# One-hots and first norm on other engines, an earlier store of the first rows, and two gathers in the other order, in a one-core layer of gated cross-attention and experts

## The reference

```
h    = layernorm(x)
q    = h @ Wq.T;  k, v = split(ctx @ Wkv.T)
# each token sees 4 rows of its batch's context: seg, seg-1, seg-2, seg-3
x    = x + tanh(g_xattn) * (softmax(q.k / 4 over the 4 rows, 16 heads) @ v) @ Wo.T
h    = layernorm(x)
p    = softmax(h @ gate_w.T); the 2 best of 8 experts
x    = x + tanh(g_ffn) * sum over them of p_e * (silu(h @ w1[e] + b1[e]) @ w2[e] + b2[e])
```

## Time and profile before

| | us |
|---|---|
| median of 3 runs | 359.64 (359.12 to 360.45) |
| the profiled execution | 359.07 |
| its span | 357.4 |
| TensorE, matmul, busy | 325.2 (91%) |
| VectorE busy | 268.8 (75%) |
| GpSimd busy | 213.9 (60%) |
| ScalarE busy | 175.9 (49%) |

### The profile page before, as it was taken

How to read it: one execution, slowest core, us unless ns; L and a number is a source line. 1 busy time by engine, 2 the same in 40 slices (tenths; PEclk the granted TensorE clock), 3 DMA queues, 4 the chain that set the end, 5 groups by cost and what they waited for, 6 DMA issues and landing times.

```text
span 357.4 us, 11383 instructions
## 1 busy us (share of the span) xinstructions
PE 325.2 (91%) x3440; PEld 269.0 (75%) x3440; DVE 268.8 (75%) x629; ACT 175.9 (49%) x495; POOL 213.9 (60%) x243
## 2 busy tenths in 40 slices
PE   8586999999999899999999999999999999999930
PEld 7455778998888688788888888888888887778720
DVE  5376899999998967878878788787887876666620
ACT  3252255555465467555565555655546553252400
POOL 4677788987675061474738747386574865662430
PEclk9897899999999989999999999999999999999985
DMA  6679999999899821122323223232332323242211
GB/s 197 203 244 420 399 422 402 415 364 406 289 386 381 271 62 33 30 40 42 61 47 51 50 43 62 47 47 48 46 61 49 48 47 62 34 65 26 33 19 14
DMA packets 31582, 53.30 MB, mean 149 GB/s; under 512 B 4882, under 2 KB 25730, under 8 KB 29476
## 3 DMA queue, kind: packets, MB, share of 16 engines
q0 software_dynamic: 9408, 26.63, 28.8%
q1 hardware_dynamic: 17700, 23.10, 18.1%
q10 hardware_dynamic: 4416, 2.80, 2.6%
HBM read 42.36 MB, written 10.17 MB: 147 GB/s over the span
## 4 chain that ended last, share of the span: by engine, by line
PE 68%; DVE 16%; issue 4%; DMA 4%; POOL 3%; ACT 2%; SPq 0%; ACTq 0%; POOLq 0%; DVEq 0%
PE ps L1246 28%; PE ps L1260 16%; PE ps L1263 8%; DVE ps L1433 4%; PE ps L1274 2%; DMA sel<-near_rows,win_near 2%; PE ps L1268 2%; PE ps L960 2%; DVE w_parts L1429 2%; PE ps L1072 2%; PE ps L1081 2%; DMA w_parts<-in_itok_BxS 2%; DVE sel L1429 2%; PE ps L1267 1%; PE ps L1262 1%
## 5 line engine op out<-in xcount | busy, mean ns | idle before, releaser
L1246 PE MATMUL ps<-sel,w_parts 128*128 128x128 f16 x1776 | 141.7, 219 | 0.8 <-issue 0.7
L1246 PEld LDWEIGHTS ps<-sel,w_parts 128*128 x1776 | 119.4, 98 | 25.9 <-issue 1.4
L939 ACT ACTIVATE sel<-ps,b1T 128x128 f32<-128x128 f32 x296 | 84.3, 368 | 89.7 <-PE ps L1246 89.6
L686 POOL DMA_INDIRECT out<-sel x37 | 62.6, 1692 | 85.0 <-DVE sel L1721 69.9
L1260 PE MATMUL ps<-w_parts,sel 128*128 x259 | 96.3, 379 | 0.3
L1263 PE MATMUL ps<-w_parts,sel 128*128 x259 | 70.6, 273 | 0.0
L678 POOL DMA_INDIRECT sel<-tokens_split,sel x37 | 43.8, 1184 | 15.7 <-DVE sel L1644 9.2
L1676 DVE SCALAR_TENSOR_TENSOR sel<-sel 128x512 f16<-128x512 f32 x74 | 51.3, 693 | 2.5
L1662 DVE SCALAR_TENSOR_TENSOR w_parts<-w_parts (+1 forms) x32 | 39.0, 1220 | 10.4 <-issue 7.2
L673 POOL TENSOR_TENSOR sel<-sel 128x1 f32<-128x1 f32 x37 | 40.2, 1086 | 2.9 <-PE ps L1274 2.9
L1674 DVE TENSOR_SCALAR sel<-sel 128x512 f16<-128x512 f32 x74 | 33.8, 456 | 8.7 <-ACT sel L939 8.2
(11 more groups left out here) (244 smaller groups left out, 479.3 us busy)
## 6 DMA issues: line engine op xcount, KB each, us to landing
w_parts<-in_L_ffn_w SPq DMA_DIRECT2D x16, 1024.0 KB, 11.4
out<-xs SPq DMA_DIRECT2D x16, 128.0 KB, 8.0
tokens_split<-xsplit ACTq DMA_DIRECT2D x13, 128.0 KB, 5.8
xs<-in_x SPq DMA_DIRECT2D x3, 512.0 KB, 8.8
near_rows<-w_parts SPq DMA_DIRECT2D x4, 256.0 KB, 6.9
sel<-tokens_split,sel POOLq DMA_INDIRECT x37, 3.0
out<-sel POOLq DMA_INDIRECT x37
w_parts<-in_L_xattn_Wkv SPq DMA_DIRECT2D x1, 512.0 KB, 4.2
```

The source lines that it names most:

```text
L686: pool.indirect_dma_start(out_rows, bass.IndirectOffsetOnAxis(slot_row[:, at(q - 1)], 0), y_sb[(k + 3) % 4], None, compute_op=ALU.add).the ...
L939: act.activation(h32[n][:, c * P:c * P + P], ps_h[n][:, c * P:c * P + P], ACT.Silu, bias=biases[:, c:c + 1], scale=1.0 / (X_SCALE * W_SCALE))\
L1246: mm = pe.matmul(ps_h[n][:, c * P:c * P + P], w, xx, start=(i == 0), stop=(i == len(products) - 1))
```

## The change

VectorE makes the one-hots, behind its flag and ahead of the token statistics of tiles 1 to 7. GpSimd's first work on data is now the first norm of tile 0, and then its part of b2. b2 is loaded on ScalarE's queue behind the tokens of batch 0, and ScalarE's copy of it stands ahead of its copies of Wkv. SyncE loads the segments for the one-hots ahead of Wkv, and the two gates, b1 and gate_w behind the tokens of batch 3. ScalarE stores the rows of batch 0. The rows of tile 1 are gathered ahead of those of tile 0. TensorE makes the first two picks, behind six spins, ahead of the transposes of Wq and the first turn, and ScalarE keeps them there.

```diff
@@ -390,8 +390,8 @@
         @block.sync
         def _(sp):
             sp.dma_start(segr_i[:, :], seg_tiles).then_inc(s["seg_in"], 16)
+            sp.dma_start(near_seg, seg_tiles[0:1, :].to_broadcast([P, P])).then_inc(s["near_in"], 16)
             sp.dma_start(wkv_raw, Wkv.rearrange("(o p) c -> p o c", p=P)).then_inc(s["wkv_in"], 16)
-            sp.dma_start(near_seg, seg_tiles[0:1, :].to_broadcast([P, P])).then_inc(s["near_in"], 16)
             sp.dma_start(wq_raw, Wq.rearrange("(o p) c -> p o c", p=P)).then_inc(s["wraw_in"], 16)
             sp.dma_start(ctx0[:, 1:B, :], ctx_first[:, 1:B, :]).then_inc(s["ctx_in1"], 16)
 
@@ -401,14 +401,6 @@
             tokens_in(1)
             sp.dma_start(wo_raw, Wo.rearrange("(o p) c -> p o c", p=P)).then_inc(s["wo_in"], 16)
             tokens_in(2)
-            sp.dma_start(gates[:, 0:1], g_xattn.rearrange("(o n) -> o n", o=1).to_broadcast([P, 1]))\
-                .then_inc(s["small_in"], 16)
-            sp.dma_start(gates[:, 1:2], g_ffn.rearrange("(o n) -> o n", o=1).to_broadcast([P, 1]))\
-                .then_inc(s["small_in"], 16)
-            sp.dma_start(b1_raw, b1.rearrange("e (c p) -> (e c) p", p=P)).then_inc(s["small_in"], 16)
-            sp.dma_start(gate_raw, gate_w).then_inc(s["small_in"], 16)
-            sp.dma_start(b2_raw, b2).then_inc(s["b2_in"], 16)
-
             def chunk(n, done, src, dst):
                 sp.dma_start(ctx_g, ctx_rows[bass.ds(src, P), :]).then_inc(s["g_ctx"], 16)
                 sp.wait_ge(s["g_kv"], n + 1)
@@ -434,9 +426,14 @@
                 sp.wait_ge(s["kv_ok"], b + 2)
                 sp.dma_start(kv_near[b], kv_sb[:, b, :]).then_inc(s[f"kv_out{b}"], 16)
 
-            near_out(0)
             sp.wait_ge(s["kv_out0"], 16)
             tokens_in(3)
+            sp.dma_start(gates[:, 0:1], g_xattn.rearrange("(o n) -> o n", o=1).to_broadcast([P, 1]))\
+                .then_inc(s["small_in"], 16)
+            sp.dma_start(gates[:, 1:2], g_ffn.rearrange("(o n) -> o n", o=1).to_broadcast([P, 1]))\
+                .then_inc(s["small_in"], 16)
+            sp.dma_start(b1_raw, b1.rearrange("e (c p) -> (e c) p", p=P)).then_inc(s["small_in"], 16)
+            sp.dma_start(gate_raw, gate_w).then_inc(s["small_in"], 16)
             near_out(1)
 
             def step(t):
@@ -523,16 +520,11 @@
             pool.iota(away_i[:, :], pattern=[[-1, WIN]], base=0, channel_multiplier=1).then_inc(s["away_ok"], 1)
             pool.wait_ge(s["away_ok"], 1)
             pool.tensor_copy(away[:, :], away_i[:, :]).then_inc(s["away_ok"], 1)
-            pool.wait_ge(s["near_in"], 16)
-            pool.tensor_copy(near_win, near_seg).then_inc(s["near_f"], 1)
-            pool.wait_ge(s["near_f"], 1)
-            pool.tensor_scalar(near_win, near_win, float(1 - WIN), 0.0, ALU.add, ALU.max).then_inc(s["near_w"], 1)
-            pool.wait_ge(s["near_w"], 1)
-            pool.wait_ge(s["away_ok"], 2)
-            for j in range(WIN):
-                pool.tensor_scalar(pick_hot[:, j, :], near_win, float(P - WIN), away[:, j:j + 1], ALU.min, ALU.is_equal)\
-                    .then_inc(s["hot_ok"], 1)
             first_norms(1, slice(0, 1))
+            pool.wait_ge(s["b2_hi_ok"], 1)
+            pool.tensor_scalar(b2_raw[:, :], b2_raw[:, :], 16.0, None, ALU.mult).then_inc(s["b2_lo_ok"], 1)
+            pool.wait_ge(s["b2_lo_ok"], 1)
+            pool.tensor_tensor(b2_lo[:, :], b2_raw[:, :], b2_hi[:, :], ALU.subtract).then_inc(s["b2_lo_ok"], 1)
             first_norms(2, slice(1, TPB))
             pool.wait_ge(s["win_ok"], 1)
             general = flag(pool)
@@ -599,15 +591,18 @@
                 pool.wait_ge(s["pick_ok"], 2)
                 pool.sem_inc(s["sel_k"], 1)
                 pool.wait_ge(s["kv_out0"], 16)
-                pool.indirect_dma_start(slot(0).rearrange("p j c -> p (j c)"), None, kv_near[0],
-                                        bass.IndirectOffsetOnAxis(win_near[:, 0:1], 0)).then_inc(s["sel_in0"], 16)
+                for u in (1, 0):
+                    pool.indirect_dma_start(slot(u).rearrange("p j c -> p (j c)"), None, kv_near[0],
+                                            bass.IndirectOffsetOnAxis(win_near[:, u:u + 1], 0))\
+                        .then_inc(s[f"sel_in{u}"], 16)
             with pool.Else():
                 pool.indirect_dma_start(slot(0).rearrange("p j c -> p (j c)"), None, kv_all,
                                         bass.IndirectOffsetOnAxis(win_all[:, 0:1], 0)).then_inc(s["sel_in0"], 16)
                 pool.wait_ge(s["sel_in0"], 16)
                 pool.wait_ge(s["pick_ok"], 2)
                 pool.tensor_scalar(keys_of(0), slot(0)[:, :, 0:D], 1.0, None, ALU.mult).then_inc(s["sel_k"], 1)
-            gather(1, 2)
+                pool.indirect_dma_start(slot(1).rearrange("p j c -> p (j c)"), None, kv_all,
+                                        bass.IndirectOffsetOnAxis(win_all[:, 1:2], 0)).then_inc(s["sel_in1"], 16)
             first_norms(3, slice(TPB, 2 * TPB))
             gather(2, 3)
             for t in range(T - 1):
@@ -620,10 +615,6 @@
                     first_norms(4, slice(2 * TPB, T))
                 elif t == 2:
                     gather(5, 6)
-                    pool.wait_ge(s["b2_hi_ok"], 1)
-                    pool.tensor_scalar(b2_raw[:, :], b2_raw[:, :], 16.0, None, ALU.mult).then_inc(s["b2_lo_ok"], 1)
-                    pool.wait_ge(s["b2_lo_ok"], 1)
-                    pool.tensor_tensor(b2_lo[:, :], b2_raw[:, :], b2_hi[:, :], ALU.subtract).then_inc(s["b2_lo_ok"], 1)
                 elif t == 3:
                     gather(6, 8)
                 elif 3 < t < T - 4:
@@ -696,11 +687,14 @@
             act.dma_start(ctx0[:, 0, :], ctx_first[:, 0, :]).then_inc(s["ctx_in0"], 16)
             act.dma_start(xs[:, 0:1, :], x_v[:, 0:1, :]).then_inc(s["x_first"], 16)
             act.dma_start(xs[:, 1:TPB, :], x_v[:, 1:TPB, :]).then_inc(s["x_in0"], 16)
+            act.dma_start(b2_raw, b2).then_inc(s["b2_in"], 16)
             act.wait_ge(s["consts"], 4)
             act.activation(var2[:, 0:1], half[:, 0:1], ACT.Copy).then_inc(s["unused"], 1)
             act.wait_ge(s["ctxT_ps"], 1)
             act.activation(ctxT[:, 0, :, :].rearrange("p k c -> p (k c)"), ps[:, 0, 0:256], ACT.Copy)\
                 .then_inc(s["ctxT_ok"], 1)
+            act.wait_ge(s["b2_in"], 16)
+            act.activation(b2_hi[:, :], b2_raw[:, :], ACT.Copy, scale=16.0).then_inc(s["b2_hi_ok"], 1)
             act.wait_ge(s["wkvT_ps"], 1)
             act.activation(WkvT[:, 0, 0:D], ps[:, 2, 0:D], ACT.Copy).then_inc(s["wkvT_ok0"], 1)
             act.wait_ge(s["wkvT_ps"], 2)
@@ -724,6 +718,8 @@
             act.wait_ge(s["seg_top_ok"], 1)
             first_x(0)
             keys_or_values(1)
+            act.wait_ge(s["kv_ok"], 2)
+            act.dma_start(kv_near[0], kv_sb[:, 0, :]).then_inc(s["kv_out0"], 16)
 
             general = flag(act)
 
@@ -803,12 +799,16 @@
                 act.wait_ge(s["shifts_ok"], n)
                 act.activation(r_ex[:, some, :], r_tmp[:, some, :], ACT.Exp).then_inc(s["rt_exp"], 1)
 
+            def picks_kept(h):
+
+                act.wait_ge(s["pick_ps"], h + 1)
+                act.activation(picked[:, 512 * h:512 * h + 512], ps[:, 2 + h, :], ACT.Copy).then_inc(s["pick_ok"], 1)
+
+            picks_kept(0)
             act.wait_ge(s["wT_ps"], 1)
             act.activation(WqT.rearrange("p k c -> p (k c)"), ps[:, 6, :], ACT.Copy).then_inc(s["wT_ok"], 1)
             first_turned(0)
-            for h in range(2):
-                act.wait_ge(s["pick_ps"], h + 1)
-                act.activation(picked[:, 512 * h:512 * h + 512], ps[:, 2 + h, :], ACT.Copy).then_inc(s["pick_ok"], 1)
+            picks_kept(1)
             first_x(1)
             first_turned(1)
             act.wait_ge(s["ctxT_ps"], 2)
@@ -827,9 +827,6 @@
             keys_values(2)
             act.wait_ge(s["small_in"], 64)
             act.activation(tanh_g[:, :], gates[:, :], ACT.Tanh).then_inc(s["gates_t"], 1)
-            act.wait_ge(s["b2_in"], 16)
-            act.activation(b2_hi[:, :], b2_raw[:, :], ACT.Copy, scale=16.0).then_inc(s["b2_hi_ok"], 1)
-
             def small_turned():
 
                 act.wait_ge(s["small_ps"], 1)
@@ -1028,10 +1025,6 @@
                         mm = pe.transpose(ps[:, bank, c * D + o * P:c * D + o * P + P], raw[:, o, c * P:c * P + P], ident[:, :])
                 mm.then_inc(s["wT_ps"], 1)
 
-            pe.wait_ge(s["seg_max_ok"], 1)
-            pe.wait_ge(s["wraw_in"], 16)
-            weight_turn(wq_raw, 6)
-
             def picks(h):
                 pe.wait_ge(s["kv_ok"], 1)
                 pe.wait_ge(s["hot_ok"], 2 * h + 2)
@@ -1112,8 +1105,12 @@
                     mm = pe.matmul(logits_at(u), x2T_at(u)[:, c, :], gateT[:, c, :], start=(c == 0), stop=(c == KC - 1))
                 mm.then_inc(s["logit_ps"], 1)
 
+            spin(6, 0)
+            picks(0)
+            pe.wait_ge(s["seg_max_ok"], 1)
```

(12 more changed lines are left out.)

## The result

| | us |
|---|---|
| the changed kernel, median of 20 runs | 360.75 (359.0 to 362.5) |
| the kernel before, timed beside it, median of 20 runs | 358.95 (356.83 to 360.45) |
| ratio | 1.0049, 95% interval 1.0029 to 1.0068 |
| span of the profiled execution, before and after | 357.4 and 360.3 |

The change made the kernel 0.5% slower, 1.8 us. The forecast was 1.5 us faster. The medians of the kernel before differ by up to 0.8 us between comparisons, so ratios are used, each taken against the kernel before on the same chip. A profile shows one execution, and the changed kernel's took 362.02 us, 1.3 above its median.

What follows compares the result with a forecast made beforehand. VectorE bounds the loop from tile 4 on, and chains through the gathers and GpSimd's list set its start. Tile 4 moves from 44.61 to 43.1, 1.5 us off the median 359.64: 358.1 us, range 355.2 to 361.4.

Steps and rivals of the forecast that it cites:

- Wkv's load: At the start, segments ahead: both loads in by 7.54, Wkv up to 2 us later, hidden by b2 at 8.9.
- The gathers: GpSimd's first two gathers: first lands after 5.7 us, second 3.9 behind, less 0.3; value product 0 starts at 26.7.
- nothing comes of it: Small loads hold both gathers up 1 us, or b2 lands near 10: tile 4 at 44.1 to 45.0, 359.6; chance 0.13.
- The rival built on a quick second gather: Tile 0's rows 1.1 us earlier, at 25.6; tile 4 at 41.0 to 42.0, 356.0 at the best; chance 0.26.
- The order of the gathers: Tile 1 starts at 24.0, 4.8 us earlier, value product 0 1.4 us later; tile 1's gain is not passed on.
- the prediction's own sum: Up to tile 4: value product 0 at 26.7, value product 1 at 33.6, tile 1's values until 37.7, tile 4 at 43.1.
- The clock: TensorE's low stretch is over by 34.7; tile 1's values take 1.95 us at full clock, until 37.7, before 39.25.
- The slow rival: Low clock covers tile 1's values, their output, batch 3's keys and values: 3.3 us; tile 4 at 46.4, 361.4; chance 0.17.

Runs made afterwards that it cites:

- the kernel with both costs taken back: Changed kernel with Wkv's load ahead of the segments again and the gathers in the order 0, 1; ratio 0.9934 to the kernel before.
- both mended: Changed kernel, segments behind Wkv, gathers 0, 1, small loads early, 60 throwaway matmuls, norms of tiles 8 to 15 ahead of tile 4's gather; ratio 0.9869, 355.18 us.
- the clock alone: Changed kernel, segments behind Wkv, gathers 0, 1, small loads early, plus 60 throwaway matmuls on TensorE behind tile 0's values; ratio 0.9905 to the kernel before.

## Why the prediction was wrong

It forecast 358.1 us with a range of 355.2 to 361.4, faster or the same in 0.85 of the cases. By the ratio the gain of 1.5 us was a loss of 1.8. Its steps:

- **Wkv's load: the step that failed.** I wrote: "swapped, both are in by 7.54, so Wkv may be up to 2 us later, which b2 hides." Wkv was in at 9.73, and b2, waited for until 7.97 and forecast for 8.9, hid nothing. I had taken the time at which both loads are in as fixed, whatever their order. A sign against it was in the trace before: the 86 GB/s from 5 to 6 us, where Wkv ends and the segments' load follows. The first Wkv copy came at 10.93, not 9.3, and TensorE's idle time, which I did not follow, put the products at half clock: their end was at 15.5, not 11.8. From there the picks needed 3.6 us, a little less than the 4.6 I gave them, and tile 0 came at 19.97, not 16.9. With Wkv first it came at 15.79, and there b2 was indeed what the Wkv copies waited for (until 8.57).
- **The gathers: mis-sized.** From the first issue to value product 0 I had 9.3 us (5.7 + 3.9 - 0.3); it took 10.5. The rival "nothing comes of it" had the cause, small loads and tokens between, as its condition, at 1 us; the runs with these loads moved show 1.8 for the small ones and 3.0 with the tokens, in the kernel with both costs taken back; whether they are also the 1.2 us missing here was not tried. By the Trainium skill ("DMA: Bandwidth & Descriptors", Anatomy of one DMA, SWDGE path) the second gather would have been in about 7 us after the first issue, an estimate; the trace has it in after 10.3 us (20.12 to 30.45). The rival built on a quick second gather did not come.
- **The order of the gathers: right in mechanism.** Tile 1 started without a wait and nothing of it was passed on; GpSimd's list bound. The steps behind the second gather were right to 0.1 us: value product 0 to value product 1 took 7.00 us, forecast 6.93; from there to tile 4 9.45, forecast 9.5. Put 30.60 into the prediction's own sum and it gives 47.0; tile 4 came at 47.05. So all of the error, 3.9 us, is in when value product 0 starts: 2.7 for the gather's later issue, 1.2 for the gathers.
- **The clock: right place.** The low stretch covered tile 0's values and was over before tile 1's, as forecast, and the full clock behind it gave back 1.4 us on the way from value product 1 to tile 4 (10.85 before, 9.45 after). The slow rival, the clock low at tile 1's values, did not happen; the slowdown came by another way, for which there was no case.
- **The rest.** The loop took 4.76 us a tile, as forecast. One-hots on VectorE, the root of tile 0's norm and b2's operations on GpSimd stand nowhere in the first 47 us of the chain that ended last; forecast for them was nothing, and no run prices them by themselves. The stored rows of batch 0 were not waited for in the changed kernel, as forecast; once the late Wkv is out of the way, the first gather waits for them. That the edits besides the two costs gain 0.66% together is shown by the run with both taken back; which of them gains it was not tried.

## What to carry to other kernels

Price a load by what it took in a trace, not by its bytes, look at what the DMA engines moved while it flowed, and ask of each load that is moved ahead of another who waits for the second: here 64 KB, one row written to 128 partitions, put 4 us on the 512 KB that TensorE, and so all the rest, was waiting for. What makes it slow is not shown: Wkv has four times as many rows, of twice the length, and no run varied the rows or read them from separate places. An edit's price holds only for the chain that binds at that moment: the same swap cost nothing measurable before, where the one-hots held the picks and the clock gave back what was left, and 0.5% after, where only the products held them. When an early gain doesn't arrive, look for the instruction in an in-order list that now waits earlier, with others queued behind it, and for the clock after the idle time; here the gain came with both mended, and with the clock alone it was within the noise.

## What the runs showed of the hardware

- A load of 64 KB, one row of 512 bytes to each of 128 partitions, landed 5.2 to 5.7 us after its issue in front of Wkv's 512 KB on the same queue, and 5.6 to 6.4 us after it behind them. In front it raised Wkv's landing from 4.2 to 4.4 us (5.4 in one kernel) to 7.9 to 8.1 us in four kernels, and the DMA engines moved 117 GB/s in two of the microseconds in which it flowed, against 225. The Trainium skill ("DMA: Bandwidth & Descriptors", Queues, rings and completion order) has each engine take the descriptors of one queue in ring order; the trace agrees: the segments were in at 6.5, Wkv at 9.7.
- The first gather of 1 MB landed 5.7 us after its issue in the kernel before. In the kernel with both costs taken back it took 9.0 us, 7.2 with the four loads of small rows issued earlier, and 6.1 at most with 512 KB of tokens and those loads both issued earlier.
- A wait of 3.8 us for a load cost at least 2 us more behind it in clock: TensorE's granted clock was 0.61 in the window in which it ended and 0.50 in the next two, and stayed at 1.00 with throwaway products in its place, where tile 0 came 2.15 us earlier.
